# Cross-attention with a routed feed-forward: 24 full blocks run ahead of the last two groups' routing, on a table of their own

## What is computed

```python
x = x + xattn(layernorm(x), ctx, ctx, mask, ...)   # 16 heads of 8, causal and key mask, softmax
x = x + ffn(layernorm(x), wg1, bg1, wg2, w_in, w_out)

# ffn, per token:
g      = gelu(xt @ wg1 + bg1);  logits = g @ wg2        # 8 experts
probs  = softmax(logits);       top 2 of them keep their probability, the rest get 0
h_e    = gelu(xt @ w_in[e])                              # 256 hidden
y      = sum over the two experts of gate_e * (h_e @ w_out[e])
```

## Time and profile before

| | |
|---|---|
| median of 3 runs | 621.63 us (619.68 to 622.26) |
| the profiled execution | 623.75 us, its span 622.0 us |
| mean granted TensorE clock | 0.956 |
| busy share of the span: PE, DVE, ACT, POOL | 81%, 77%, 63%, 40% |
| chain that ended last, by engine | DVE 35%, PE 34%, issue 13%, SP's queue 9% |

### The profile page before, as it was taken

How to read it: one execution, slowest core, us unless ns; L and a number is a source line. 1 busy time by engine, 2 the same in 40 slices (tenths; PEclk the granted TensorE clock), 3 DMA queues, 4 the chain that set the end, 5 groups by cost and what they waited for, 6 DMA issues and landing times.

```text
span 622.0 us, 18994 instructions
## 1 busy us (share of the span) xinstructions
PE 501.8 (81%) x6640; PEld 377.4 (61%) x6640; DVE 481.1 (77%) x1629; ACT 393.0 (63%) x723; POOL 248.8 (40%) x323
## 2 busy tenths in 40 slices
PE   2579898888888888888888887411999999999992
PEld 0146555555554554554555554301999999999992
DVE  3588999999999999999999997660566666566662
ACT  2156687777777777777777676511666666566660
POOL 4131233353353354254254233340355555455552
PEclk9999999999999999999999999555999999999997
DMA  3137212212212212212110101047233334333310
GB/s 110 18 81 220 62 48 69 78 42 66 81 40 65 83 39 65 83 40 62 46 41 26 52 20 38 35 137 241 76 107 103 109 105 110 98 110 86 80 42 1
DMA packets 41805, 46.87 MB, mean 75 GB/s; under 512 B 9738, under 2 KB 33555, under 8 KB 41248
## 3 DMA queue, kind: packets, MB, share of 16 engines
q1 hardware_dynamic: 33696, 30.39, 18.7%
q0 software_dynamic: 5984, 12.90, 6.1%
q10 hardware_dynamic: 2032, 2.36, 1.3%
HBM read 28.54 MB, written 18.58 MB: 76 GB/s over the span
## 4 chain that ended last, share of the span: by engine, by line
DVE 35%; PE 34%; issue 13%; SPq 9%; DMA 2%; ACT 2%; POOL 1%; ACTq 0%; another core or an unknown queue 0%; POOLq 0%; DVEq 0%
PE probs_t L562 14%; PE bank L573 13%; DVE smax L776 9%; DVE rden L788 7%; SPq L266 5%; DVE rows L798 2%; PE scores L553 2%; DVE left L843 2%; DVE sm L780 1%; SPq L238 1%; DVE stat L753 1%; DVE stat L804 1%; DVE xT L763 1%; PE scores L377 1%; PE probs_t L393 1%
## 5 line engine op out<-in xcount | busy, mean ns | idle before, releaser
L1174 POOL DMA_INDIRECT out<-yb,token_row x91 | 89.3, 982 | 106.2 <-DVE yb L1059 65.9
L1136 POOL DMA_INDIRECT routed_rows<-rows,pos x64 | 64.3, 1004 | 122.5 <-DVE pos L879 100.9
L678 ACT ACTIVATE pt<-probs_t 128x1024 f32<-128x1024 f32 x64 | 65.5, 1023 | 60.0 <-PE probs_t L393 59.7
L717 ACT ACTIVATE hb<-probs_t 128x512 f32<-128x512 f32 x91 | 54.3, 597 | 73.2 <-PE probs_t L562 54.9
L562 PE MATMUL probs_t<-xbT,wi 128*128 128x128 f32 x728 | 98.1, 278 | 2.3 <-ACT wi L732 1.2
L377 PE MATMUL scores<-kx,qT 64*64 64x512 f32 x512 | 70.6, 621 | 36.2 <-DVE sm L780 23.9
L573 PE MATMUL bank<-wo,hb 128*128 x728 | 96.1, 275 | 0.0
L562 PEld LDWEIGHTS probs_t<-xbT,wi 128*128 128x128 f32 x728 | 90.1, 195 | 3.1 <-issue 1.7
L573 PEld LDWEIGHTS bank<-wo,hb 128*128 128x128 f32 x728 | 88.5, 192 | 0.1
L776 DVE TENSOR_REDUCE smax<-scores 128x16 f32<-128x1024 f32 x64 | 77.8, 1216 | 12.2 <-PE scores L383 10.9
L780 DVE TENSOR_TENSOR sm<-scores,smax 128x1024 f32<-128x1024 f32 x64 | 78.4, 1224 | 2.2
(11 more groups left out here) (117 smaller groups left out, 838.3 us busy)
## 6 DMA issues: line engine op xcount, KB each, us to landing
xb<-routed_rows SPq DMA_DIRECT2D x91, 132.5 KB
ctx_in<-ctx_t SPq DMA_DIRECT2D x16, 256.0 KB, 3.0
x_all<-x SPq DMA_DIRECT2D x16, 256.0 KB, 3.3
kx<-kT SPq DMA_DIRECT2D x256, 16.0 KB
routed_rows<-padding_rows SPq DMA_DIRECT2D x15, 132.5 KB
routed_rows<-padding_rows ACTq DMA_DIRECT2D x14, 132.5 KB
out<-yb,token_row POOLq DMA_INDIRECT x91
mask_in<-mask SPq DMA_DIRECT2D x16, 64.0 KB, 3.8
```

The lines of the kernel that those rows point to most:

```text
L678: nc.scalar.activation(pt[:, :, :].rearrange("p j q -> p (j q)"), PT2[:, :], ACT.Copy).then_inc(s_ptev, 1)
L1136: nc.gpsimd.indirect_dma_start(out=rows_d, out_offset=bass.IndirectOffsetOnAxis(ap=pos[:, r % RR, u:u + 1], axis=0), in_=rows[:, r % RR, u ...
L1174: nc.gpsimd.indirect_dma_start(out=out, out_offset=bass.IndirectOffsetOnAxis(ap=token_row[:, b % RY:b % RY + 1], axis=0), in_=yb[:, b % RY ...
```

## The change

The work on rows of the first 13 groups is cut off as a part of its own. 13 groups are 6656 tokens; whatever their bins, they hold at least 24 full blocks.

- **First table.** In stage 15, when group 12 is counted, DVE computes the number of full blocks per bin (rounded down), and a table for the first NA = 24 of them. PE turns it in the same stage; it uses the bank W0. Then DVE moves the start of each bin behind the rows taken.
- **Blocks 0 to 23** run after the attention from this table. SP waits only for the scatters of groups 0 to 12.
- **The gating of groups 14 and 15** is cut into steps, `last_gates(b)`, which each engine runs after its work on block b: logits and choice of 14 at b = 0, transposes, rank, count and positions at 3, hidden of 15 at 5, logits and choice at 7, rank, count, `tails`, positions at 10, the second table at 11, 12, 13 (PE) and 14. POOL scatters group 14 ahead of output 4 and group 15 ahead of output 12.
- **Paddings** are all issued by SP, 14 ahead of the loads of group 4 of blocks (16 to 19) and 14 ahead of group 5 (20 to 23), each as 16 pieces of 8 rows instead of 128 of one. SP waits for their landing and the last scatters ahead of block 24.
- **Blocks 24 to 90** run from the second table.
- After the last stage, the normalisation of tile 63 comes ahead of the count and positions of group 13, and PE's last projection ahead of the transposes of group 14.
- x lies in a ring of 6 groups (`x_in`), its load waits for the residual of the group six before; the ring `xb` has 10 slots instead of 8, `yb` 10 instead of 6.

```diff
+EARLY = 13
+NA = 24
+PART_OF = (0, NA)
+NBS = (NA, NB - NA)
+RR_X = 6
+PADS_BEFORE = (4, 5)
-RX = 8
+RX = 10
-RY = 6
+RY = 10
+SCATTER_AT = (4, 12)
...
                 def load_x(s):
-                    sp.dma_start(x_all[:, s * U:(s + 1) * U, :], x_r[:, s * U:(s + 1) * U, :]).then_inc(s_x[s % RING], 16)
+                    if s >= RR_X:
+                        sp.wait_ge(s_res, U * (s - RR_X + 1))
+                    sp.dma_start(x_in[:, s % RR_X, :, :], x_r[:, s * U:(s + 1) * U, :]).then_inc(s_x[s % RING], 16)
...
+                            sp.dma_start(rows_d[bass.ds(at, BLK), :].rearrange("(a r) w -> a (r w)", a=16),
+                                         pad_c.ap().rearrange("(a r) w -> a (r w)", a=16)).then_inc(s_pad, 16)
...
-                sp.wait_ge(s_tails, 1)
-                pad_regions(mybir.EngineType.SP, sp, PAD_SP)
-                sp.wait_ge(s_tabd, 1)
                 for g in range(len(GROUPS)):
+                    if g in PADS_BEFORE:
+                        if g == PADS_BEFORE[0]:
+                            sp.wait_ge(s_tails, 1)
+                        half = PADS_BEFORE.index(g)
+                        pad_regions(range(half * NP // 2, (half + 1) * NP // 2))
                     load_group(g)
...
@@ PE
+                        if u == 2 and s == NS - 1:
+                            turn_table(0)
...
+                def last_gates(b):
+                    if b == 0:
+                        pe.wait_ge(s_res, NT)
+                        gate_logits(NS - 2)
+                    if b == 3:
+                        pe.wait_ge(s_rge, NS - 1)
+                        transpose_rows(NS - 1)
+                        pe.wait_ge(s_lsh, NS - 1)
+                        rank_tokens(NS - 2)
+                    if b == 5:
+                        gate_hidden(NS - 1)
+                    if b == 7:
+                        pe.wait_ge(s_pch, CNT * (NS - 2) + 2)
+                        gate_logits(NS - 1)
+                    if b == 10:
+                        pe.wait_ge(s_lsh, NS)
+                        rank_tokens(NS - 1)
+                    if b == 13:
+                        turn_table(1)
...
                         down(b, experts[2 * (b - first):2 * (b - first) + 2])
+                        last_gates(b)
@@ ACT
+                def last_gates(b):
+                    if b == 0:
+                        gate_exp(NS - 2)
+                        ln2_norm(NS - 1)
+                    if b == 3:
+                        xt2_evac(NS - 1)
+                    if b == 5:
+                        gate_gelu(NS - 1)
+                    if b == 7:
+                        gate_exp(NS - 1)
...
                         if b > 1:
                             gelus(b - 2)
+                            last_gates(b - 2)
                         copy_w_in(b, experts[2 * (b - first):2 * (b - first) + 2])
@@ DVE
                             positions(s - 3)
+                            if s == EARLY + 2:
+                                dve.wait_ge(s_cum, 1)
+                                blocks_of_bins(0)
+                        if u == 1 and s == EARLY + 2:
+                            ends_of_bins(0)
+                            bins_of_blocks(0)
+                        if u == 3 and s == EARLY + 2:
+                            write_tables(0)
+                            start_second_part()
...
+                normalise(NT - 1)
                 residual(NT - 2)
                 count_tokens(NS - 3)
                 positions(NS - 3)
-                normalise(NT - 1)
                 residual(NT - 1)
...
+                def last_gates(b):
+                    if b == 0:
+                        choose(NS - 2)
+                    if b == 3:
+                        count_tokens(NS - 2)
+                        positions(NS - 2)
+                    if b == 7:
+                        choose(NS - 1)
+                    if b == 10:
+                        count_tokens(NS - 1)
+                        dve.wait_ge(s_pch, CNT * (NS - 1) + 2)
                         nc.vector.tensor_copy(tails[:, :], run_s[:, :]).then_inc(s_tails, 1)
-                    positions(r)
-                make_tables()
-                dve.wait_ge(s_tabd, 3)
+                        positions(NS - 1)
+                    if b == 11:
+                        blocks_of_bins(1)
+                        ends_of_bins(1)
+                    if b == 12:
+                        bins_of_blocks(1)
+                    if b == 14:
+                        write_tables(1)
...
                     gated(b)
+                    last_gates(b)
@@ POOL
                 for b in range(NB):
+                    if b in SCATTER_AT:
+                        r = NS - 2 + SCATTER_AT.index(b)
+                        rows_complete(r)
+                        scatter_rows(r, range(U))
                     scatter_out(b)
```

More of the change, by code:

```diff
@@ L44 @@
 RW = 2 * D + E + 1
-ROUND = float(1 << 23)
+ROUND = float(3 << 22)
 CH = 9
@@ L226, in build @@
         s_tok, s_part = (sem(n) for n in ("token_rows_ready", "first_expert_added"))
[L227 to L238, removed]
         (s_bt, s_bte, s_up, s_gl, s_dn, s_gm, s_gt, s_yb) = (sem(n) for n in (
@@ L313, in _, with pad_regions @@
                     body(s, s // 2, s % 2)
+                def pad_regions(bins):
+                    for first in range(bins.start, bins.stop, NP // 4):
+                        _, values = nc.values_load_multi_w_load_instructions(
+                            tails[0:1, first:first + NP // 4], engines=[mybir.EngineType.SP], min_val=0, max_val=ROWS - BLK,
+                            skip_runtime_bounds_check_because="made on the chip by counting into existing regions")
+                        for k in range(NP // 4):
+                            start = (first + k) * REG
+                            at = nc.s_assert_within(values[k], start, start + N,
+                                                    skip_runtime_bounds_check_because="a region holds all tokens")
+                            sp.dma_start(rows_d[bass.ds(at, BLK), :].rearrange("(a r) w -> a (r w)", a=16),
+                                         pad_c.ap().rearrange("(a r) w -> a (r w)", a=16)).then_inc(s_pad, 16)
                 def load_group(g):
-                    first, n = GROUPS[g]
+                    p, first, n = GROUPS[g]
+                    if first == PART_OF[p]:
+                        sp.wait_ge(s_tabd, 3 * p + 1)
                     _, values = nc.values_load_multi_w_load_instructions(
@@ L472, in rank_tokens, with turn_table @@
                     last.then_inc(s_rank, 1)
+                def turn_table(p):
+                    pe.wait_ge(s_spread, p + 1)
+                    for k in range(3):
+                        last = nc.tensor.transpose(TABLE[p][:, k * P:(k + 1) * P], spread_out[:, k, :], ident[:, :])
+                    last.then_inc(s_tabp, 1)
                 def body(s, i, par):
@@ L736, in _ @@
                 act.wait_ge(s_wo, 32)
-                act.wait_ge(s_tabd, 2)
-                for g, (first, n) in enumerate(GROUPS):
+                for g, (p, first, n) in enumerate(GROUPS):
                     experts = experts_of(g)
@@ L1164, in body @@
                             add_positions(s + 3)
-                        if u == 3 and runs(s, 3):
+                        if u == 3 and runs(s, 3, NS - 2):
                             scatter_rows(s - 3, (3,))
```

166 lines of the change are left out of this document (80 added, 86 removed).

## The result

The changed kernel takes 626.85 us (median of 4 runs, 624.98 to 629.0), the kernel before 620.75 (4 runs, 619.68 to 622.26): 1.0086 times as long, 95% interval 1.0053 to 1.0118. It is slower by 0.9%, inside the predicted range of 609 to 629, but the forecast case (619.7) fell, and what happened is the mechanism of the rival *SP decides* (627, chance 0.27).

A forecast was written before the change was run, and what follows sets the result against it. DVE was taken to bound attention, PE the expert blocks, with a hole between as target. Terms -30.7 (start), +18.8 (gating), +7.9 (padding), +2.1 (clock) sum to -1.9 us, giving 619.7; own range 613 to 624, all cases 609 to 629.

The forecast's parts named there:

- the forecast case: Whole kernel: the prediction's own main case, 619.7 us, with its own range of 613 to 624; chance 0.45.
- SP decides: SP's paddings before blocks 16 and 20: 0.68 us each, 13 us of waits, 4.2 for clock drops, 627 us; chance 0.27.
- start of the blocks: After attention: the first up matmul starts at 401.9 instead of 433.48, a term of -30.7 us.
- gating up to down(13): Gating of groups 14 and 15 run in line under the blocks: 17.4 us of a +18.8 us term.
- block 14, padding and clock, down(13) to down(24): Later early blocks: 1.4 us for gating at block 14, 7.9 for padding waits, 2.1 for one clock drop.
- The holes foreseen behind the first and the eighth down: Sign on PE under the gating: a hole of about 6 us after the first down, 3 after the eighth.
- far from 19 us: Sign of being wrong: the sum of PE's waits up to block 16 is far from 19 us.
- The padding: SP's 28 paddings before blocks 16 and 20: 0.54 us each, 10.0 a half, making PE wait +7.9 us.
- The waits: PE waiting for loads of blocks 16 and 20: 4.4 and 3.5 us, or 6.5 each at 0.68 per padding.
- The clock: PE's granted clock: halved after one of the two waits at blocks 16 and 20, a loss of +2.1 us.
- Table loads cost double: ACT's four switches in blocks 0 and 7 each hold it twice as long: 5.2 us more, 625; chance 0.03.
- Early table fails to start early: SP still waits for a late scatter: blocks start some 10 us later, gain gone, 630 us; chance 0.03.

The follow-up runs named there:

- e2: Changed kernel with the paddings back in 128 pieces of one row, still all by SP: 635.77 to 650.07 us, 1.0200 of the kernel before.
- e13: Changed kernel with 18 idle PE matmuls ahead of the transpose of block 20 alone: 627.38 us, 1.0104 of the kernel before.
- e8: Changed kernel with both halves of the padding one group of loads later, as in e1, run again: 621.55 us, 1.0020 of the kernel before.
- e6: Changed kernel with gating steps and scatters at earlier blocks and the second half of the padding in quarters: 613.61 us, 0.9899 of the kernel before.
- e1: Changed kernel with both halves of the padding issued one group of loads later: 640.87 us, too scattered for a ratio.
- e4: Changed kernel with the gate's exp of groups 14 and 15 replaced by a linear function, leaving out four table loads: 638.82 us, 1.0222 of the kernel before.
- e9: Changed kernel with all gating ahead of block 0 and paddings in quarters, earlier: 619.83 us, 0.9879 of the kernel before.
- e12: The linear gate for groups 14 and 15 in the changed kernel, as in e4, run again: 638.68 us, 1.0147 of the kernel before.
- e3: Changed kernel with 60 and 36 idle PE matmuls ahead of the transposes of blocks 16 and 20: 643.88 us, 1.0304 of the kernel before.
- e11: The same idle PE matmuls as e3 in the changed kernel, run again: 641.29 us, 1.0201 of the kernel before.

## Why the prediction was wrong

By its own steps, predicted against measured, within the traces:

| step | predicted | measured |
|---|---|---|
| start of the blocks | -30.7, first up 401.9 | -32.2, first up 400.93 |
| gating up to down(13) | 17.4 of the 18.8 | 42.8 - 13 x 1.9 = 18.1 |
| block 14, padding and clock, down(13) to down(24) | 1.4 + 7.9 + 2.1 = 11.4 | 39.0 - 20.8 = 18.2 |
| sum at down(24) | -1.9 | +4.1 |

**The start of the blocks** was right, to 1.5 us (the prediction's own terms add up to 401.6 and not 401.9). The first table came where it was foreseen; the row maxima of stage 15 ran some 3 us late, of the 2 to 4 foreseen.

**The gating** was right to 0.7 us in its price, and nearly piece by piece. Against 1.9 us a block, block 0 with the clock behind it cost 7.1 (foreseen 6.0 and 0.9), block 3 2.0 (2.1), 5 1.7 (1.7), 7 to 9 4.4 (3.2), 10 to 13 2.9 (3.5). The one drop of the clock not foreseen here is behind block 7: down(8) takes 2.07 us instead of 1.06. But two things in it were wrong, and that the price came out is in part luck. The holes foreseen behind the first and the eighth down, 6 and 3 us, are 3.58 and 1.94 (and 0.42), and PE's holes of over 0.8 us up to down(13) sum to 9.8 where the prediction set "far from 19 us" as a sign of being wrong; the rest of the price is PE's own work, much of it at half clock. And in block 0 the prediction put the table load and the gelu, 1.88 us, on PE's path, where up(2) and a transpose at half clock, 2.1 us, stand instead and cover them.

**The padding** is the step that failed. PE came to block 16 at 451.0, where the forecast had 450.9, and waited 7.36 us for its rows instead of 4.4. The step reads: "A half costs two register loads (1.15 to 1.48 each, I take 1.2) and 14 issues" at 0.54. Measured are 0.68 per padding and 0.94, 1.81, 1.48 and 1.48 us for the register loads. The first half takes 12.5 instead of 10.0 us, the second 12.8, and the two together shift block 20 by 5.3 of the 6.2 us by which its transpose (474.0) is later than forecast (467.8); the rest is in the block loads between and behind them, less the 0.3 by which `tails` came early. The 0.54 was chosen against the only padding rows there were, on the argument that the DMA engines, at 0.96 to 1.0, had slowed the issues. The traces speak against it: the issue is 0.497 us in 16 pieces and, in e2, in 128. The 0.54 belongs to a load into SBUF, of which a single issue takes 0.33 us (median of 91 in the changed kernel); a copy from DRAM to DRAM of the same bytes issues in 0.50. The prediction itself named the turning point, a half over some 11 us, and both halves are beyond it.

**The waits** were where they were placed: 7.36 and 4.85 us, with 4.4 and 3.5 in the forecast case and 6.5 twice in the rival. The rival's 6.5 is 0.9 short of the first, as the register loads were longer still, and 1.7 over the second. By the prediction's own steps 0.68 gives 6.4 and 5.5 us, not 6.5 twice.

**The clock** fell once at each of the two waits, as in the rival. But the rival's 4.2 us count one drop too many. The chain from `tails` over 28 paddings to the load of block 20 lies on SP alone, whatever PE does meanwhile, so what PE lost at half clock after block 16 came off the wait at 20. Only the second drop, 1.9 us, stands behind that wait. This is worked out from the traces: from `tails` to the transpose of block 20 it is 31.5 us in the changed kernel and 31.5 in e13, whose PE does 4.2 us of other work in between. The medians of e13 don't show it, so it isn't settled to the microsecond. That the rival's number fits is therefore in part luck, with too much in its waits and drops and too little in its register and block loads; its mechanism is what came true.

**The sum** of measured terms: -32.2 + 18.1 + 18.2 = +4.1 at down(24). By the last blocks 1.5 of it is gone, since blocks 24 to 80 took 107.7 us in the trace of before and 106.2 here, with the same instructions; 56 blocks at 1.9 are 106.4. That is part of the 3.0 by which before's profiled execution lay over its median. The medians, 6.1 us apart, are nearest the rival's +5.3; what lies between them and the +4.1 isn't traced to a term.

*Table loads cost double* is refuted by ACT's timeline (nothing stands between the load and the gelu), *Early table fails to start early* by the first up at 400.93. *SP decides* is borne out by e8, which moves only the paddings, one group later (5.4 us better), by e2, which changes only their form (the same waits), and by e6, where they come earlier, in quarters and behind earlier gating (13.3 us better).

The Trainium skill (DMA: Bandwidth & Descriptors, Issuing engines are not separate DMA queues) says that issuing from several engines saves only the sequencer's time to start a DMA, which is usually small beside the DMA itself. Taken one by one that holds in this trace, 0.50 us of issue beside 2.2 from issue to landing of a block load of the same size; but 28 starts in one queue held SP for 25 us, and that decided the time.

## What to carry to other kernels

Price a DMA that is moved onto another queue by its own row, issue and spacing and address registers together, and not by a DMA with the same bytes; then ask what stands behind it in that queue and how many blocks cover it. When work is pulled into a hole, put the longest serial part of it (here `tails` and the paddings behind it) first, for here the last step decided, and what stood in line under the blocks cost about what it costs alone. Between two waits on one queue, a delay of the consumer after the first went into the second here; only what stands behind the last one counted.

## What was not expected of the hardware

**Several engines standing still at once.** On the one chip of e1 to e4 and e9 to e12 the kernel before took 624.92 and 628.22 us, where it took 620.22 and 621.02 in the other two rounds. The same instructions of one kernel in both, as ACT's timeline has them, first e1, then e8:

```profile
429.93 0.37 ACT L699 ACTIVATE hid_s<-bank,bg_s 128x128 f32<-128x128 f32 x1 [6.96 <-remote]
```

```profile
423.86 0.37 ACT L699 ACTIVATE hid_s<-bank,bg_s 128x128 f32<-128x128 f32 x1 [2.69 <-PE bank L465]
```

In e1 DVE's next copy (428.36) also waited 3.26 us for something the profile calls remote, and PE's hole was 5.36 us instead of 1.08. A hole of 5.3 to 5.4 us stands at the same place in e2, e3, e4, e11 and e12. These five, all with the changed kernel's order of steps, took 1.5 to 3% more than the kernel before there, the changed kernel 1% elsewhere. The cause wasn't tried and stays open.

**Register loads**, both from SBUF, differ by a factor of three to six: 0.94 to 1.81 us for `tails` and 0.30 for the addresses of block loads. The first bring seven values and the second four, which may account for a part; it wasn't tried.

**A filler on PE**, 128x128 by 128x128 in float32, is two records, 0.227 us together at full clock; e3 and e11 were spoilt by counting one.
